# A second attention whose order is changed: maxima two steps earlier, x scaled at step 0, one pass of modulation on ScalarE, q and k turned in two halves

## What is computed

```python
x, emb                                   # x (8, 256, 512), emb (8, 1, 512)
scale, shift = split(emb @ W_emb + b_emb)
xn  = rms_norm(x, g_norm) * (1.0 + scale) + shift
q, k, v = heads(xn @ W_qkv)              # 16 heads of 32
q, k = rms_norm(q, g_q), rms_norm(k, g_k)
attn = softmax(q @ k.T * 32 ** -0.5)
o = attn @ v
return o + o @ W_out
```

## Time and profile before

| | us |
|---|---|
| three runs, median | 2002.25 (2002.22 to 2002.59) |
| the profiled execution | 1989.18 |
| its span | 1987.5, mean granted TensorE clock 0.913 |
| second attention in it, with its loads | about 853 to 1396 |
| one batch in the middle of it | 57.8 to 61.6 |

### The profile page before, as it was taken

One profiled execution on the slowest core, in us unless ns is written; L12 is line 12 of the kernel. 1 busy time (PEld: TensorE's weight loads), 2 busy tenths in 40 slices (PEclk: granted clock), 3 DMA queues, 4 the chain that ended last, 5 costly groups with the idle time before them and its releaser, 6 DMA issues. The chain is left out here.

```text
span 1987.5 us, 31522 instructions
## 1 busy us (share of the span) xinstructions
PE 1654.1 (83%) x10250; PEld 959.7 (48%) x10250; DVE 1083.0 (54%) x2020; ACT 581.2 (29%) x1096; POOL 275.9 (14%) x343
## 2 busy tenths in 40 slices
PE   5788888888248899755778888887899999999998
PEld 1132333232124455442344444444777777777776
DVE  4455656553555445325355655563566666666665
ACT  0333433444323223123344334342111121121121
POOL 4211111011542123211111101110000000000000
PEclk7899999999579999955798989988899999999999
DMA  5422211111597999461111101110850000000000
GB/s 161 146 60 60 59 43 41 34 43 51 182 296 140 203 197 245 76 216 32 32 44 44 37 17 32 44 43 23 139 109 1 11 11 0 11 11 0 11 11 11
DMA packets 195488, 145.43 MB, mean 73 GB/s; under 512 B 126492, under 2 KB 163120, under 8 KB 195336
## 3 DMA queue, kind: packets, MB, share of 16 engines
q1 hardware_dynamic: 179000, 109.84, 21.7%
q0 software_dynamic: 15632, 34.30, 8.0%
q10 hardware_dynamic: 768, 0.13, 0.0%
HBM read 50.95 MB, written 41.56 MB: 47 GB/s over the span
## 5 line engine op out<-in xcount | busy, mean ns | idle before, releaser
L1866 PE MATMUL d_bank<-XTh,d_wgu 128*128 (+1 forms) x1408 | 244.7, 273 | 0.0
L1953 ACT ACTIVATE d_SG<-d_bank 128x256 f32<-128x256 f32 x264 | 101.4, 384 | 381.6 <-PE d_bank L1866 301.8
L329 DVE TENSOR_REDUCE W<-a_bn 128x1 f32<-128x512 f32 x256 | 163.5, 686 | 85.5 <-PE a_bn L243 82.1
L2015 DVE SCALAR_TENSOR_TENSOR d_HF<-d_bank,d_SG 128x256 f32<-128x256 f32 x264 | 112.2, 425 | 171.0 <-ACT d_SG L1953 152.7
L1866 PE MATMUL d_bank<-XTl,d_wgu 128*128 (+1 forms) x704 | 192.4, 273 | 0.0
L311 ACT ACTIVATE W<-a_bt 128x512 f32<-128x512 f32 x256 | 144.1, 596 | 152.9 <-PE a_bt L262 151.9
L1866 PEld LDWEIGHTS d_bank<-XTh,d_wgu 128*128 128x128 f16 x1408 | 138.2, 98 | 18.0
L280 PE MATMUL a_bc<-W 128*64 128x512 f32 x512 | 142.7, 637 | 0.0
L243 PE MATMUL a_bn<-W 97*128 97x512 f16 x256 | 99.8, 422 | 48.1 <-DVE W L329 28.5
L1113 PE MATMUL b_G<-W,R 128*128 x468 | 79.7, 322 | 53.2 <-issue 53.2
L2022 DVE TENSOR_TENSOR d_H_l<-d_HF,d_H_h 128x256 f16<-128x256 f32 x264 | 112.4, 426 | 9.0
(11 more groups left out here) (286 smaller groups left out, 3050.8 us busy)
## 6 DMA issues: line engine op xcount, KB each, us to landing
W<-W SPq DMA_DIRECT2D x96, 64.0 KB, 3.0
W<-W POOLq DMA_DIRECT2D x96, 64.0 KB, 2.6
W<-in_x SPq DMA_DIRECT2D x8, 512.0 KB, 3.8
W<-W SPq DMA_DIRECT2D x32, 128.0 KB
x<-x_rows SPq DMA_DIRECT2D x8, 512.0 KB, 11.7
c_a_A<-c_H SPq DMA_DIRECT2D x64, 64.0 KB, 3.1
c_a_B<-c_H POOLq DMA_DIRECT2D x64, 64.0 KB, 2.8
c_a_CT<-c_a_CS SPq DMA_DIRECT2D x32, 128.0 KB
```

Of the source, the lines that this page charges most:

```text
L329: self.nc.vector.tensor_reduce(self.NM[:, s * cols:(s + 1) * cols], self.bn[s % 2][:, :].rearrange("p (k n) -> p k n", k=cols), AX, ALU.ma ...
L1866: mm = MM(b[:, w * CH:(w + 1) * CH], wgu[:, f, w, KF * s + k, :], X[m][:, k, toks], start=(w == 0 and k == 0 and i == 0), stop=(k == KF - ...
L1953: nc.scalar.activation(SG[k % 3][:, :], GU[(f + 3) % 4][:, 0:CH], ACT.Silu, scale=1.0 / WS).then_inc(silu, 1)
L2015: V.scalar_tensor_tensor(out=HF[:, :], in0=b[:, CH:2 * CH], scalar=1.0 / WS, in1=SG[k % 3][:, :], op0=ALU.mult, op1=ALU.mult).then_inc(mul ...
```

## The change

Four edits, all in `layer1_attention`:

1. `lag` goes from 8 to 6. Before, each of steps 8 to 15 has two maxima. After, step 6 has two, 7 two, 8 one, 9 two, 10 one, 11 two, 12 two, 13 one, 14 two, 15 one.
2. `xs` moves from step 3 to step 0, ahead of `recip` and `spread`.
3. ACT makes only the f32 `XN`. DVE makes `XNh` from it with a cast in SBUF, then subtracts. The PSUM bank is given back when `XN` is there.
4. `qk` is cut into `qk0` (q) and `qk1` (k). The end of a batch was shift, v0, qk, v1; it is qk0, shift, v0, qk1, v1.

```diff
-    c = Core(heads=16, ..., lag=8, shift_scale=1.0, n_post=4, n_early=2)
+    c = Core(heads=16, ..., lag=6, shift_scale=1.0, n_post=4, n_early=2)
...
-        plan = c.plan(7, {1: ("recip",), 2: ("spread",), 3: ("xs",), 5: ("xt0", "xt1", "out"), 7: ("q0",), 8: ("k0",),
+        plan = c.plan(7, {0: ("xs",), 1: ("recip",), 2: ("spread",), 5: ("xt0", "xt1", "out"), 7: ("q0",), 8: ("k0",),
...
-                      ("shift", "v0", "qk", "v1"))
+                      ("qk0", "shift", "v0", "qk1", "v1"))
...
-                def pre_qk(n, uses):
+                def pre_qk(n, uses, w):
                     pe.wait_ge(qn_done, n.idx + 1)
-                    for w in range(2):
...
                     act.sem_inc(begun, 1)
-                    for dst in (XN, XNh[n.par]):
-                        for k in (2 * u, 2 * u + 1):
-                            ins = nc.scalar.activation(dst[:, k, :], bank[:, (k - 2 * u) * S0:(k - 2 * u + 1) * S0],
+                    for k in (2 * u, 2 * u + 1):
+                        ins = nc.scalar.activation(XN[:, k, :], bank[:, (k - 2 * u) * S0:(k - 2 * u + 1) * S0],
...
-                    ins.then_inc(xn_hi, 1)
+                    ins.then_inc(xn_made, 1)
...
-                    dve.wait_ge(xn_hi, 2 * n.idx + u + 1)
+                    dve.wait_ge(xn_made, 2 * n.idx + u + 1)
                     dve.sem_inc(a.proj_out, 1)
                     ks = slice(2 * u, 2 * u + 2)
+                    V.tensor_copy(XNh[n.par][:, ks, :], XN[:, ks, :]).then_inc(xn_hi, 1)
+                    dve.wait_ge(xn_hi, 2 * n.idx + u + 1)
                     V.tensor_tensor(XNl[n.par][:, ks, :], XN[:, ks, :], XNh[n.par][:, ks, :], ALU.subtract).then_inc(xn_done, 1)
```

More of the change, by code:

```diff
@@ L1652, in scale, with pre_qk @@
                     V.tensor_tensor(qk, qk, ssq[:, :].unsqueeze(2).to_broadcast([P, 64, D]), ALU.mult).then_inc(qn_done, 1)
-                def pre_qk(n, uses, chain):
-                    for w in range(2):
-                        for u in range(2):
-                            bank = a.taken(dve, uses)
-                            dve.wait_ge(qk_hi, 4 * n.idx + 2 * w + u + 1)
-                            ks = slice(2 * u, 2 * u + 2)
-                            chain.did(V.scalar_tensor_tensor(out=L[w][:, ks, :], in0=bank[:, :].rearrange("p (k s) -> p k s", k=2),
-                                                             scalar=gcol[:, w:w + 1], in1=H[w][:, ks, :],
-                                                             op0=ALU.mult, op1=ALU.subtract))
-                            chain.wait(dve)
-                            dve.sem_inc(a.proj_out, 1)
-                    dve.sem_inc(a.split_done, 1)
+                def pre_qk(n, uses, chain, w):
+                    for u in range(2):
+                        bank = a.taken(dve, uses)
+                        dve.wait_ge(qk_hi, 4 * n.idx + 2 * w + u + 1)
+                        ks = slice(2 * u, 2 * u + 2)
+                        chain.did(V.scalar_tensor_tensor(out=L[w][:, ks, :], in0=bank[:, :].rearrange("p (k s) -> p k s", k=2),
+                                                         scalar=gcol[:, w:w + 1], in1=H[w][:, ks, :],
+                                                         op0=ALU.mult, op1=ALU.subtract))
+                        chain.wait(dve)
+                        dve.sem_inc(a.proj_out, 1)
+                    if w == 1:
+                        dve.sem_inc(a.split_done, 1)
                 def spread(n, uses, chain):
```

47 lines of the change are left out of this document (23 added, 24 removed).

## The result

The changed kernel took 1982.55 us (median of four executions, 1973.96 to 1986.03) beside 2002.24 for the kernel before: a ratio of 0.9916, 95% interval 0.9893 to 0.9939. A second set gave 1980.51 beside 2000.29, 0.9903 (0.9884 to 0.9922). So it is faster by 17 to 20 us, where 4.7 were forecast; 1982.55 lies outside the predicted range of 1991 to 2009. Two slow executions further down, of 2300.75 and 6814.37 us, are left out of the medians there.

A forecast was written before the change was run, and what follows sets the result against it. PE was taken to bound the kernel, with waits and half-clock spells in its time. Waits and work summed to −2.3 and the clock to −2.4, so −4.7 from 2002.25: 1997.6 us, range 1991 to 2009.

The forecast's parts named there:

- The head: Head of batches 1 to 5: spread waits 0.5 more, x's transposes 1.08 less, W_out 0.9 less; −6.4 us in all.
- batch 0's wait: Batch 0: PE's 3.98 wait for exponentials becomes 1.8 shorter, the maxima's work adds 0.5; −1.3 us.
- The middle: Steps 6 and 7, five batches: third maximum waits 1.25, fourth 0.35, plus 0.55 of moved work; +10.8 us.
- moved matmuls: Two maxima leave the last steps, where PE waits for DVE ahead of shift anyway; 0.55 us per batch.
- The end: End of batches 0 to 5: scaling 0.6 earlier, q's transposes first, second values 0.96 earlier per batch; −5.8 us.
- The clock's term: Batches 1 to 5: half-clock spells removed, −3.4 and −2.4, against new ones, +3.4; −2.4 us.
- New idle places: Ten new or longer idle places, at spread and step 7 in five batches, charged two half-clock spells; +3.4 us.
- One sign: Mean granted clock stays at 0.91 to 0.92.
- The other sign: Forecast is wrong if the clock of batches 1 to 5 leaves its 0.86 to 0.91.
- The rival in which the clock gains all: All half-clock spells gone, none new: −2.3 − 8.5 = −10.8, 1992 us; chance 0.2, shared with a smaller middle stall.
- That of the starved clock: Step 7 stall and spread wait let the clock fall at all ten places: +8.9, 2011 us; chance 0.12.
- The rival of the transposes: q's transposes ahead of first values keep the clock low, one more spell per batch: +6.2, 2008.5 us; chance 0.1.

The follow-up runs named there:

- the two edits: Kernel before with only the scaling of x at step 0 and the single ACT pass of modulation: 1988.7 us beside 1999.5, ratio 0.9957.
- the run with the maxima alone: Kernel before with only the maxima two steps earlier (lag 8 to 6): 2001.3 us beside 1999.5, ratio 1.0015.
- the new order: Kernel before with only q and k turned in two halves around shift and first values: 1983.9 us beside 1999.5, ratio 0.9923.
- the first profile of before: Unchanged kernel before, the profiled execution that the prediction was read from: 1989.18 us.
- The second profile: Kernel before run again with no edit: 1998.55 us, its profiled execution 1997.77 us.
- the fill of W_out's wait alone: Kernel before with 15 useless matmuls ahead of W_out: 1981.4 us beside 1998.1, ratio 0.9916.
- the order with the transposes ahead: Kernel before with q and k turned undivided ahead of shift and values: 1982.2 us beside 2000.3, ratio 0.9912.
- the batch that ran wholly at the full clock: Batch 4 of the kernel before with 12 useless matmuls ahead of the 13th maximum and 10 ahead of the last products: 1978.6 us, ratio 0.9904.
- filled transposes: Kernel before with 3, 7, 3 and 5 useless matmuls ahead of transpose rounds of q and k and the second values: 1990.2 us, ratio 0.9960.
- the order with the transposes ahead with the shorter head: Kernel before with scaling at step 0, single pass, and q and k turned undivided ahead of shift and values: 1981.5 us beside 1998.4, ratio 0.9912.
- the single pass alone: Kernel before with only the single modulation pass on ACT, the f16 copy cast on DVE: 1979.2 us beside 1998.4, ratio 0.9914.
- the two filled kernels without the earlier maxima: Changed kernel without earlier maxima, useless matmuls added ahead of W_out, 13th maximum and last products: 1973.5 us; at more places, only where waits cover them: 1965.3 us.
- the best order: Changed kernel with the earlier maxima undone (lag 8): 1966.6 us beside 2000.3, ratio 0.9846; repeated, 1967.7 us.

## Why the prediction was wrong

**The head was right.** The spread waits 0.58 (0.5 predicted), the wait for the scaled x is gone, W_out waits 0.92 (0.9), batch 0's wait fell by 1.82 (1.8). Idle time of the two edits: −5.4 to −5.7 where −6.4 stood. Batch 0 as a whole isn't shorter for it: 56.1 us, at a clock of 0.78, beside 54.5 (0.89) and 56.6 (0.84) before.

**The middle was right in its waits** (1.30 and 0.21; 1.25 and 0.35 predicted) and in the 0.55 of moved matmuls, which showed at the last products (1.75 instead of 1.15, 2.9 in all) and not ahead of shift.

**The end was wrong in size.** −0.96 per batch came from chaining transposes, low parts and banks from the scaling's end, by rows of batch 0 at the full clock. Two things are different in the batches that count. PE isn't free when the scaling ends (1180.78 + 2.28 = 1183.06): it is at the last products and begins q's transposes at 1184.18, and it does so in the spell that every batch has there. So v0 starts 5.1 after the scaling, not 3.5. And 0.6 of the 0.96 was credit for the scaling that comes earlier with the maxima. PE is held at the last products by the exponentials, 0.6 longer than before (the run with the maxima alone has that wait too), so an earlier scaling frees nothing. Alone, the new order changes PE's idle time by +0.8 to +1.1 in five batches; the −4.8, without the credit −1.8, isn't there.

**Together, without the clock,** the terms of batches 1 to 5 summed to −0.4; measured, idle time rose by 1.7 to 2.0. An error of 2. So the waits, mis-sized or not, aren't the gain. Nor is the scatter of executions: the second set gave the gain again, and its profile has the same five batches (290.8 long, 238.7 busy).

**The clock's term was wrong, and it is the result.** It stood at −2.4. PE's busy time in batches 1 to 5, the same instructions, fell by 9.9 against the first profile of before and by 14.7 against the second. That the direction came out as forecast is luck in part: the waits, which were to give half of the 4.7, gave nothing that the profiles show, and the clock gave it all. Three steps in its term failed:

1. The spells were counted in one execution, which turned out to be one of the fastest of its kernel. The second profile has more of them (79 us at half clock against 66), and with the same waits in both a median of 1999.5 to 2002 makes as many as there, or more, likely. The 13 us between the profiled execution and the median should have been read as a warning that the count was not typical, and not carried over as a constant. Of the 8.6 us between the two profiled executions 6 lie in batches 0 to 7. The count also left out a spell in the head of batch 2, 5 us into it.
2. New idle places were charged two spells. The stretch with the stall at step 7 stayed at 1.00 in batch 3, and batches 2 to 5 have no spell ahead of the end; batch 1 has one, in its head. So one spell at most stands against the two.
3. Each spell was laid to the wait right ahead of it. The fills show that idle places do let the clock fall: the fill of W_out's wait alone took 16.7 us off. But much of that came from the spell at the end of the batch, 30 us further on. The wait ahead of W_out at its full 1.82 had no spell in the order with the transposes ahead, nor in the batch that ran wholly at the full clock, and at 0.92 it had spells ahead of it. A wait is an occasion, and whether it becomes a spell depends on where the others stand.

One sign that the prediction set failed to show this: the mean granted clock of the whole execution was 0.912 after and 0.913 before in the first pair of profiles (0.916 and 0.908 in the second). Batch 0 and stretches outside the eight batches had less of it. The other sign did show it: batch 5 left the 0.86 to 0.91 with 0.94.

The rival in which the clock gains all came nearest, with 1992 and −8.5 for the clock. That of the starved clock is refuted in its place, step 7. The rival of the transposes is refuted as well: the first values run behind q's transposes in the spell that was there anyway, and k's transposes, from 1192.36 on, ran at 1.00. The rule of the Trainium skill that was set beside it (TensorE: Matmul & The Clock Gate, Part 4: PE-mode transpose) fits one thing here, that the spell of 13.7 covers all transposes when they stand together, though it begins 3.8 us ahead of the first of them. That filled transposes lose their spell fits it too. But neither run parts transposes from the waits between them.

**What stays open.** In some kernels one batch length repeats, and it is one of few. Near 58.0 repeat the change (three batches), the order with the transposes ahead with the shorter head (three) and without it (all five), and the single pass alone (three), though their five-batch idle times are 52.1, 40.5, 47.9 and 43.8. Near 61.4 repeat the earlier maxima alone (61.27 in batch 3) and two batches of the second profile of before (61.51, 61.43), and near 54.8 the two filled kernels without the earlier maxima. These lengths lie 3.2 to 3.4 apart, about as much as the shortest spell lasts. Other kernels repeat none: the first profile of before, the scaling and pass, the kernel before with the turning filled. So where the length holds, waits that are saved come back as half clock; that is shown for the one pair of orders with the transposes ahead. It would explain why the parts don't add up: the scaling and the pass alone are −6.8 and −19.1, together −10.8; the earlier maxima alone cost 1.8, in the whole 10 to 14. (The three parts alone, +1.8, −10.8 and −15.6, sum to −24.6 where the whole gives −19.7, which is within their intervals.) What makes a batch settle on one length rather than another isn't settled by these runs. Nor is all of the gain seen in a trace: batches 0 to 7 took 431.7 and 437.7 in the two profiles of before, 424.1 and 424.2 after, so 7.5 to 13.6 of the 17 to 20; outside these batches the four executions took 1557 to 1562. Within the eight batches the difference is busy time alone: PE's idle time is 77.8 and 77.4 before, 77.6 and 77.7 after. The timed executions leave no trace, and the rest of the gain is put to the same spells only by argument.

## What to carry to other kernels

Where the granted clock falls in spells, the time of a change is not the sum of its waits: take the busy time of the bounding engine for the same instructions as a second account, keep in mind that slow work hides waits, and count spells in more than one execution before a price is put on them. An order that puts thin work together, inside a spell that is there anyway, can be worth more than one that removes a wait; here it gave 18.1 on the kernel before, but only 6 on top of the shorter head, where the same work in halves gave 19 to 23. So try parts alone and together. And a wait that can't be removed may be filled: useless matmuls gained 7.9 to 19.4 us in waits of the kernel before, gave nothing clear on the best order, and lost 6.8 in two batches where, it seems, no wait covers them.
